# Order of the first loads and constants of a graph kernel, and conversions of edge groups between two engines

## What is computed

```python
def _spmm(row, col, val, x):
    return jax.ops.segment_sum(val[:, None] * x[col], row, num_segments=N)
...
xn = _layernorm(x, axis=-1)
x = x + _L0_gnn_ref(xn, W0, b0, W1, b1, edge_weight, src, dst) + _L0_mix_ref(xn[None], wq, wk, wv, wo, ...)[0]
x = x + _L0_ffn_ref(_layernorm(x, axis=-1)[None], gate_w, gate_b, w1, b1, w2, b2)[0]
```

## Time and profile before

| what | us |
|---|---|
| median of 3 runs | 1198.19 (1196.59 to 1199.76) |
| the profiled execution, whole | 1198.36 |
| its span, first to last instruction | 1196.6 |
| PE busy | 1111.3 (93%) |
| DVE busy | 702.7 (59%) |
| ACT busy | 320.5 (27%) |
| POOL busy | 167.7 (14%) |

### The profile page before, as it was taken

One profiled execution on the slowest core, in us unless ns is written; L12 is line 12 of the kernel. 1 busy time (PEld: TensorE's weight loads), 2 busy tenths in 40 slices (PEclk: granted clock), 3 DMA queues, 4 the chain that ended last, 5 costly groups with the idle time before them and its releaser, 6 DMA issues.

```text
span 1196.6 us, 14106 instructions
## 1 busy us (share of the span) xinstructions
PE 1111.3 (93%) x4909; PEld 703.5 (59%) x4909; DVE 702.7 (59%) x1566; ACT 320.5 (27%) x1035; POOL 167.7 (14%) x202
## 2 busy tenths in 40 slices
PE   4789989999999999999989999999999299999995
PEld 2456656666666666666674444545568266666664
DVE  7998989998776877868730110224347324444443
ACT  3557767411212112222210101201112022222220
POOL 1113222300101110100000000000333401111111
PEclk9789989999999999999998999999999599999998
DMA  5100111123333333422248988787982553344410
GB/s 171 12 14 40 45 45 45 45 89 124 123 124 124 123 124 124 154 102 88 88 185 307 361 299 299 280 295 267 310 297 107 178 169 114 116 144 135 147 40 7
DMA packets 65861, 175.39 MB, mean 147 GB/s; under 512 B 16607, under 2 KB 49146, under 8 KB 53758
## 3 DMA queue, kind: packets, MB, share of 16 engines
q1 hardware_dynamic: 53950, 123.74, 30.2%
q10 hardware_dynamic: 7520, 42.68, 8.8%
q0 software_dynamic: 4320, 8.04, 1.9%
HBM read 113.82 MB, written 63.01 MB: 148 GB/s over the span
## 4 chain that ended last, share of the span: by engine, by line
PE 79%; DVE 9%; issue 3%; ACT 2%; another core or an unknown queue 2%; SPq 1%; DMA 1%; POOL 1%; POOLq 0%; DVEq 0%; ACTq 0%
PE ps L1437 20%; PE ps L1587 18%; PE ps L1420 11%; PE ps L1693 9%; PE ps L1682 9%; PE ps L1343 2%; PE ps L1404 2%; PE ps L1463 2%; PE ps L1390 2%; DVE W L952 1%; PE ps L1439 1%; ACT W L680 1%; SPq L428 1%; ACT W L764 1%
## 5 line engine op out<-in xcount | busy, mean ns | idle before, releaser
L1437 PE MATMUL ps<-RING,XX 128*128 128x512 f32 x600 | 282.8, 594 | 0.3 <-ACT RING L708 0.3
L1587 PE MATMUL ps<-RING,RY 128*128 128x512 f32 (+2 forms) x750 | 277.3, 526 | 4.7 <-issue 4.7
L1587 PEld LDWEIGHTS ps<-RING,RY 128*128 128x128 f32 x750 | 134.0, 192 | 131.2 <-issue 129.0
L1420 PEld LDWEIGHTS ps<-RING 128*128 128x128 f32 x1250 | 163.7, 193 | 45.8 <-issue 44.7
L708 ACT COPY RING<-ps 128x512 f32<-128x512 f32 (+1 forms) x157 | 91.7, 584 | 316.7 <-PE ps L1420 300.4
L1420 PE MATMUL ps<-RING 128*128 128x128 f32 x1250 | 171.1, 278 | 0.5 <-ACT RING L698 0.5
L1437 PEld LDWEIGHTS ps<-RING,XX 128*128 128x128 f32 x600 | 102.9, 191 | 72.9 <-issue 71.7
L992 DVE TENSOR_TENSOR RING<-iota_n,RY 128x512 f32<-128x512 f32 (+1 forms) x157 | 107.9, 688 | 42.1 <-PE ps L1420 38.9
L998 DVE TENSOR_TENSOR RING<-iota_n,RY 128x512 f32<-128x512 f32 (+1 forms) x157 | 117.1, 746 | 0.0
L1001 DVE TENSOR_TENSOR RING<-RING,RY 128x512 f32<-128x512 f32 x132 | 90.0, 682 | 0.0
L1325 DVE SCALAR_TENSOR_TENSOR W<-ps,RING,W 128x256 f32<-128x256 f32 (+1 forms) x32 | 15.5, 484 | 122.1 <-PE ps L1693 121.2
(11 more groups left out here) (244 smaller groups left out, 1261.2 us busy)
## 6 DMA issues: line engine op xcount, KB each, us to landing
RING<-adj_dram SPq DMA_DIRECT2D x62, 1280.0 KB, 6.3
adj_dram<-RING ACTq DMA_DIRECT2D x31, 1280.0 KB, 4.5
XT<-in_L_ffn_w SPq DMA_DIRECT2D x8, 1024.0 KB, 7.8
RING<-in_L_ffn_w SPq DMA_DIRECT2D x8, 1024.0 KB, 6.6
rbuf_dram<-W SPq DMA_DIRECT2D x8, 516.0 KB, 5.3
RING<-rbuf_dram SPq DMA_DIRECT2D x8, 516.0 KB, 3.8
xbuf_dram<-W SPq DMA_DIRECT2D x8, 512.0 KB, 3.3
RING<-xbuf_dram SPq DMA_DIRECT2D x8, 512.0 KB, 4.7
```

Of the source, the lines that this page charges most:

```text
L1420: last = nc.tensor.matmul(o[:, i * P:(i + 1) * P], h[:, 0, i, :], h[:, 1, i, :], start=True, stop=(j != s))
L1437: last = nc.tensor.matmul(ps[:, ACC + dd, :], w, at, start=(j == 0), stop=True, skip_group_check=True)
L1587: last = nc.tensor.matmul(o, (Y if l == 0 else S0)[:, j, :], RING[:, slot_of[g % 5], i * across + first:i * across + first + w], start=(j ...
```

## The change

Ten edits, in the order of the engines' starts:

1. ACT issues x for tiles 0 to 6 first, then `wk` and `wv`.
2. The eleven small constants leave ACT and go to SP, behind the windows of group 1 (tiles 2 to 5) and ahead of the windows of group 2. They still count on `s_w`.
3. SP issues the windows of group 0 without a loop.
4. SP issues x for tiles 7 to 24 ahead of the five weights.
5. DVE samples `dst` before it makes `iota_s`, `cen` and `fresh`.
6. ACT makes `before`, `ident_b`, `own_b` and `upto_b` (it was DVE), while it waits for `wk` and `wv`.
7. POOL fills `ones_b`, two columns of `khat` and `vacc` (it was DVE).
8. The remaining gate constants are made by DVE between the variances and the refinement of tiles 0 to 6 (`gate_constants`).
9. PE waits for ACT's and POOL's constants too (`s_constb`, `s_fill`); ACT no longer waits for DVE's.
10. For groups 1 to 3 ACT makes the three conversions, one turn of the loop ahead (`cast`, at it = 1, 5 and 15). DVE's `prepare` waits for them (`s_cast`), and `cast` waits until the group before has been read (`s_prepared`).

```diff
@@ sync
             for g, (t0, t1) in enumerate(GROUPS):
-                with sp.Fori(t0, t1) as j:
-                    first = sp.value_load(base_i[0:1, ds(j, 1)], min_val=0, max_val=E - WIN)
...
                 if g == 0:
-                    for to, src in ((wo_n, half("L0_mix_wo")), (wq_n, half("L0_mix_wq")), (W0_n, a["L0_gnn_W0"]),
-                                    (W1_n, a["L0_gnn_W1"]), (b1_n, a["L0_ffn_b1"])):
+                    for j in range(t0, t1):
+                        window(g, j)
+                else:
+                    with sp.Fori(t0, t1) as j:
+                        window(g, j)
+                if g == 1:
+                    for to, src in ((gate_w[:, :, :], half("L0_ffn_gate_w")), (bo_b[:, :], a["L0_mix_bo"].partition_broadcast(P)), (gb1_b[:, :], a["L0_gnn_b1"].partition_broadcast(P)),
...
                         sp.dma_start(to, src).then_inc(s_w, 16)
...
+                if g == 0:
+                    for to, src in ((wo_n, half("L0_mix_wo")), (wq_n, half("L0_mix_wq")), (W0_n, a["L0_gnn_W0"]),
+                                    (W1_n, a["L0_gnn_W1"]), (b1_n, a["L0_ffn_b1"])):
+                        sp.dma_start(to, src).then_inc(s_w, 16)
@@ gpsimd
+            gp.wait_ge(s_blk, 3)
+            gp.memset(ones_b[:, :], 1.0).then_inc(s_fill, 1)
+            for i in range(2):
+                gp.memset(khat[i][:, 2:4, P:P + 1], 1.0).then_inc(s_fill, 1)
+            gp.memset(vacc, 0.0).then_inc(s_fill, 1)
+            gp.wait_ge(s_fill, 4)
@@ scalar
+            act.dma_start(X1[:, 0:XG[0][1], :], a["x"][0:XG[0][1] * P, :].rearrange("(j p) d -> p j d", p=P)).then_inc(s_x[0], 16)
             act.dma_start(wk_n, half("L0_mix_wk")).then_inc(s_kvw, 16)
             act.dma_start(wv_n, half("L0_mix_wv")).then_inc(s_kvw, 16)
-            act.dma_start(X1[:, 0:XG[0][1], :], a["x"][0:XG[0][1] * P, :].rearrange("(j p) d -> p j d", p=P)).then_inc(s_x[0], 16)
-            for to, src in ((gate_w[:, :, :], half("L0_ffn_gate_w")), (bo_b[:, :], a["L0_mix_bo"].partition_broadcast(P)), (gb1_b[:, :], a["L0_gnn_b1"].partition_broadcast(P)),
...
+            act.wait_ge(s_const, 9)
+            nc.scalar.copy(before[:, :], before_f).then_inc(s_constb, 1)
+            nc.scalar.copy(ident_b[:, :], ident[:, :]).then_inc(s_constb, 1)
+            nc.scalar.activation(own_b[:, :], ident[:, :], ACT.Copy, scale=OWN).then_inc(s_constb, 1)
+            nc.scalar.copy(upto_b[:, :], upto[:, :]).then_inc(s_constb, 1)
...
+            def cast(g):
+                t0, t1 = GROUPS[g]
+                n, m = slice(t0 * WC, t1 * WC), slice(0, (t1 - t0) * WC)
+                act.wait_ge(s_win[g], 16 * 3 * (t1 - t0))
+                act.wait_ge(s_prepared, g)
+                nc.scalar.copy(srcf[:, m], src_w[:, n]).then_inc(s_cast, 1)
+                nc.scalar.copy(dstf[:, m], dst_w[:, n]).then_inc(s_cast, 1)
+                nc.scalar.copy(pay[:, t0 * C2:t1 * C2, 2, :], val_w[:, n].rearrange("p (c i) -> p c i", i=2)).then_inc(s_cast, 1)
...
+                if it + 1 in starts:
+                    cast(starts.index(it + 1))
@@ vector, prepare
-                v.tensor_copy(srcf[:, m], src_w[:, n])
-                v.tensor_copy(dstf[:, m], dst_w[:, n])
...
+                if g == 0:
+                    v.tensor_copy(srcf[:, m], src_w[:, n])
+                    v.tensor_copy(dstf[:, m], dst_w[:, n])
+                    link(v.tensor_copy(field(2), pairs(val_w[:, n])))
+                else:
+                    dve.wait_ge(s_cast, 3 * g)
@@ vector, start
             stats(0)
             variances(0)
+            gate_constants()
             scales(0)
@@ tensor
+            pe.wait_ge(s_constb, 4)
+            pe.wait_ge(s_fill, 4)
             pe.wait_ge(s_constv, 1)
             pe.wait_ge(s_base, 1)
```

More of the change, by code:

```diff
@@ L294, in graph_program @@
         s_cen = sem("s_cen")
+        s_fill = sem("s_fill")
+        s_cast = sem("s_cast")
+        s_prepared = sem("s_prepared")
+        s_constb = sem("s_constb")
         s_zero = sem("s_zero")
@@ L651, in _ @@
                 nc.scalar.copy(wkvT[:, c, :], ps[:, 4 + c, :]).then_inc(s_wtc, 1)
-            act.wait_ge(s_constv, 1)
             def others_out():
@@ L722, in _ @@
                 normal(j)
+            starts = [t0 for t0, _ in GROUPS]
             for it in range(NU + 3):
@@ L871, in _ @@
             v.tensor_copy(iota_k[:, :], ints[:, 160:160 + 2 * P])
-            v.tensor_copy(iota_s, ints[:, 416:416 + SW])
-            v.tensor_scalar(fresh, ints[:, 900:900 + SW], 1.0, None, ALU.min)
-            dve.wait_ge(s_const, 9)
-            dve.wait_ge(s_blk, 3)
-            v.tensor_tensor(cen, blk, ident[:, :], ALU.add).then_inc(s_cen, 1)
             dve.wait_ge(s_dst, 16)
@@ L881, in _ @@
             v.tensor_reduce(cnt, cmp.rearrange("p (j k) -> p j k", k=17), AX_X, ALU.add).then_inc(s_cnt0, 1)
+            v.tensor_copy(iota_s, ints[:, 416:416 + SW])
             dve.wait_ge(s_tot0, 1)
@@ L884, in _, with gate_constants @@
             v.tensor_scalar(base_i[:, :], base_f, 0.0, float(E - WIN), ALU.max, ALU.min).then_inc(s_base, 1)
-            v.tensor_copy(before[:, :], before_f)
-            v.tensor_copy(ident_b[:, :], ident[:, :])
-            v.tensor_scalar(own_b[:, :], ident[:, :], OWN, None, ALU.mult)
-            v.tensor_scalar(iota_e[:, :], ints[:, 32:32 + NE], 1.0 / NE, None, ALU.mult)
-            v.tensor_scalar(last_e[:, :], ints[:, 32:32 + NE], float(XS), float(CAPX - 1), ALU.mult, ALU.add)
-            link(v.memset(base_b[:, :], 0.0))
-            v.tensor_scalar(base_b[0:1, :], ints[0:1, 32:32 + NE], float(XS), None, ALU.mult)
-            v.memset(base_b[32:33, :], -1.0)
-            v.tensor_copy(upto_b[:, :], upto[:, :])
-            v.memset(ones_b[:, :], 1.0)
-            for i in range(2):
-                v.memset(khat[i][:, 2:4, P:P + 1], 1.0)
-            v.memset(vacc, 0.0)
-            v.memset(zpad[:, :], 0.0)
-            v.engine_nop().then_inc(s_constv, 1)
-            dve.wait_ge(s_constv, 1)
+            dve.wait_ge(s_const, 9)
+            dve.wait_ge(s_blk, 3)
+            v.tensor_tensor(cen, blk, ident[:, :], ALU.add).then_inc(s_cen, 1)
+            v.tensor_scalar(fresh, ints[:, 900:900 + SW], 1.0, None, ALU.min)
+            def gate_constants():
+                v.tensor_scalar(iota_e[:, :], ints[:, 32:32 + NE], 1.0 / NE, None, ALU.mult)
+                v.tensor_scalar(last_e[:, :], ints[:, 32:32 + NE], float(XS), float(CAPX - 1), ALU.mult, ALU.add)
+                link(v.memset(base_b[:, :], 0.0))
+                v.tensor_scalar(base_b[0:1, :], ints[0:1, 32:32 + NE], float(XS), None, ALU.mult)
+                v.memset(base_b[32:33, :], -1.0)
+                v.memset(zpad[:, :], 0.0)
+                v.engine_nop().then_inc(s_constv, 1)
+                dve.wait_ge(s_constv, 1)
             def prepare(g):
```

26 lines of the change are left out of this document (13 added, 13 removed).

## The result

| what | before | after |
|---|---|---|
| median, us | 1198.19 (1196.59 to 1201.27, 5 runs) | 1204.28 (1203.13 to 1205.03, 4 runs) |
| the profiled execution, whole | 1198.36 | 1203.13 |
| its span | 1196.6 | 1201.4 |

The ratio on record is 1.0037 of the time before, interval 1.0022 to 1.0053. (It is not the quotient of the two medians, which is 1.0051; the two profiled executions give 1.0040.) So the kernel is slower by about 0.4%, where no difference was forecast, and its time is above the range. One further execution, at 1314.73 us and a granted clock of 0.857 instead of 0.96 to 0.97, is left out.

The account below looks back on a forecast made before the run. DVE was taken as bounding the start, its shift carried to the end; 1.55 us later at `scales(1)` and 1.8 back at groups 2 and 3 gave −0.25, 1198.36 to 1198.1 us, range 1194.4 to 1202.2.

Parts of the forecast that it names:

- What bounds the kernel: DVE from its restart at 45.75 to about 80 us has no gap, so what shifts 45.75 shifts the end.
- `base_i` at 7.2: Head, DVE: sampling `dst` earlier gains 0.7 us (0 to 1.4), so `base_i` comes near 7.2 instead of 7.88.
- wk, wv and the root: Head: wk and wv land at 8.8, PE starts 1.4 us later, root near 14.1, `prepare(0)` 0.7 us later at 15.6.
- Everything behind them on SP stands 2.0 us earlier: SP after group 0's windows: x issued at 11.4, last window of group 1 issued at 28.2 instead of 30.20.
- rival D: SP's issues at 16 to 21 us stay held, group 1's windows come no earlier; 1.7 us later, 1200.1; chance 6%.
- the gain of 1.8 at L945: `prepare(1)`: group 1's windows land at 29.6, so DVE goes on at 30.2 instead of 31.98.
- `s_w` full at 35.3: Eleven constants on SP: issued from 28.5 in 5.0 us, landing 1.7 later, full at 35.3 (34.0 to 38).
- Rival C: Constants' issue on SP keeps ACT's price, 7.0 us; `s_w` full after 37; 3.6 us slower or more, 1202; chance 20%.
- From there to DVE's restart, 12.0: From full `s_w` through PE and ACT to the second root: 12.0 us, restart at 47.3 against 45.75.
- Groups 2 and 3, gain 1.8: Later groups: conversions of 0.60 and 1.19 us leave DVE for ACT; gain 1.8 us (0.8 to 1.8).
- Rival B: PE's late start is not felt and DVE never held; 3.6 us won, 1194.8; chance 24%.

Follow-up runs that it names:

- e4: The kernel before with only ACT making the three conversions of groups 1 to 3; 1190.09 us, ratio 0.9994 to the kernel before.
- e1: The changed kernel with the eleven constants counted on their own semaphore, so PE's others() waits for the five weights alone; 1192.60 us, ratio 1.0018 to before.
- e8: The changed kernel with the eleven constants back on ACT and the three conversions back on DVE; 1198.70 us, ratio 0.9990 to the kernel before.
- e6: Changed kernel, but constants behind group 3's windows on own count, weights behind group 1's, ACT issuing x of tiles 7 to 24, wk/wv first; 1194.27 us, ratio 0.9960.

## Why the prediction was wrong

**What bounds the kernel: right.** DVE's restart behind the second root was the point, and its shift, +5.68, went on unchanged to turn 4 (+5.70). There was one gap that I had not seen, DVE's 0.32 us for ACT at 58.72; most of the 0.42 that came back after turn 4 is this.

**`base_i` at 7.2: wrong, small.** 7.94. The list lands when it lands: issued at 0.80, it came 5.04 later, and the order of DVE's steps no longer mattered. I had let it land at 4.9, though I wrote that x now moves in the same bytes.

**wk, wv and the root: right.** PE began at 9.20 (said 8.8), the root fell at 13.97 (14.1), `prepare(0)` at 15.46 (15.6), `stats(1)` at 19.36 without a wait (19.6).

**"Everything behind them on SP stands 2.0 us earlier": this step failed, in all its parts.** `base_i` was to give 0.7: the first window was issued at 9.11 instead of 9.09. The missing loop was to give 1.3: from there to the next transfer passed 3.47 us (9.11 to 12.58) instead of 4.32, so it gave 0.85. x was thus issued 0.83 us earlier, not 2.0. And the 0.83 were lost again behind x, where I had let every issue move along unchanged: the windows of group 1 ended at 30.22, not 28.2. Before, part of the hold behind x was covered by SP's start of the loop, and now `wo` fills it. I had written the hold down as rival D and given it 6%, although the exchange of x and weights was in front of me. This took the gain of 1.8 at L945 (30.2 said, 32.33 found) and moved the constants by 1.9 (30.44 instead of 28.5). How much the exchange alone costs was not run.

**`s_w` full at 35.3: 38.78, the step that made the sign.** Of the 3.5 us, 1.9 are the queue that did not come earlier; 0.8 is the issue (5.8 us instead of 5.0; the last four take 0.6 each); 0.7 is the landing (2.5 us from the end of the last issue, where I had taken 1.8). Each stood among my bounds, and 38 was my upper end; what I missed is that D and C add. I gave them as rivals with 6% and 20% and a price each (1200.1 and 1202), while the case that came is both at once.

**From there to DVE's restart, 12.0: right, 0.65 short.** 12.65 (38.78 to 51.43), with both steps at the lower clock as said.

**Groups 2 and 3, gain 1.8: half a microsecond too much.** 0.59 (said 0.60) and 0.67 (said 1.19), and the same in e4. I had taken the second from a stretch of three steps without asking why one of them lasted 0.72. That late windows might hold ACT was right, but I bounded it at 1 us; with the first wait taken away ACT stands 5.04 us and DVE 4.66 (e1). In the changed kernel it is covered.

**The sum with the measured terms:** 5.70 − 0.42 − 0.59 − 0.67 = 4.0 later, 1202.4; the profiled run took 1203.13. Between them lie shifts that no edit accounts for: +0.24 between turns 6 and 10 (DVE's wait for ACT there was 1.78 us instead of 1.52), −1.2 from turn 16 to 24, and +1.7 behind it.

**Rival B** (PE's late start is not felt) is refuted by DVE's wait of 3.61 us for the root. **Rival C** was right in place and in its condition (later than 37), and 1202 was nearest of all to the result. Its issue price was too high, though (7.0 us, 5.8 found): `s_w` came after 37 because the queue had not come earlier, too.

The Trainium skill (DMA: Bandwidth & Descriptors, "Issuing engines are not separate DMA queues") says that a second issuing engine only saves issue time, "which is usually small relative to the DMA itself". For one load that agrees with the trace: the last constant took 0.60 us to issue and 3.09 from there to landing. But the eleven issues stand in one queue and add up to 5.8 us, and what stands behind them in that queue pays for all of them.

## What to carry to other kernels

Count what an issuing queue does as work on the path, transfer by transfer, and look at who stands behind: small loads that nobody needs soon belong behind the last urgent ones, on a counter of their own. A gain in front of a wait is worth only as much as the awaited transfer comes earlier, so find out first what holds that transfer's issue (here large loads ahead of it in the same queue). When two rivals can happen together, price them together.

## What I had not expected of the hardware

- An issue can take 2.32 us (3.11 in e8) instead of 0.4 when 2.3 MB are ahead of it in its queue and the DMA engines are full (331 GB/s, share 1.03). In all ten kernels with x on SP, the issue behind x ended 5.0 to 5.9 us after x's first issue had begun.
- Small loads behind large ones of another queue land late: windows of 9 KB that took 1.7 us were waited for until 16.65 in e6, 4.5 us after the issue of the last had ended.
- Eleven small loads landed 3.1 to 3.75 us after the start of their last issue, with nothing large beside them and whichever stood last.
